# Byte masks of the quantised weights moved from VectorE to ScalarE, down steps that wait for the remainders only at their last product, and rewritten orders

## The chip, the cores and the metric

The kernel runs on one core of one Trainium2 chip. The metric is the device time of one execution in microseconds. It was run three times; the median is 339.18 us. TensorE (PE) does the matmuls, VectorE (DVE), ScalarE (ACT) and GpSimd (POOL) the element-wise work, and SyncE's queue (SP) issues nearly all DMAs. Each engine works through its own instruction list in order and meets the others at semaphores.

## The reference, cut to what matters

Two transformer layers on four sequences of 256 tokens with 256 features, each: attention, residual, layer norm, gated feed-forward, residual, layer norm.

```
x = layernorm(x + L0_attn(x));  x = layernorm(x + L0_ffn(x))     # 32 query heads of 8, 8 key heads
x = layernorm(x + L1_attn(x));  x = layernorm(x + L1_ffn(x))     # 16 query heads of 16, 8 key heads

# layer 0's feed-forward: weights rounded to float8_e4m3fn and back
wq = w.astype(float8_e4m3fn).astype(float32);  y = (x @ wq) * scale
# layer 1's feed-forward: weights are looked up, w = lut[idx], 16 entries
h = silu(gate(x)) * up(x);  out = down(h)
```

## The kernel before, in words

**Jobs.** A job j is one sequence in one layer: jobs 0 to 3 are layer 0, jobs 4 to 7 layer 1. Each job is cut into steps. TensorE's are q and kv (projections), max (scores only to find each query's maximum, 16 units a job in layer 0, 8 in layer 1), mt (turns the maxima), score (scores again, with the maximum subtracted), pv (probabilities times values), turn, back, wo (the end of attention), tr (turns x), gu (gate and up, six chunks) and down (six chunks). Every step has partner steps on other engines: VectorE reduces the maxima (max) and forms the hidden chunk (gu), ScalarE does the exponentials (score), the tanh (gu) and most copies out of PSUM, GpSimd forms remainders.

**Split operands.** To keep float32 accuracy, a rounded part and a remainder are multiplied separately. For the hidden chunk i of the down product, ScalarE writes the rounded part HH (step hsplit, semaphore `h_hi`), then GpSimd subtracts and writes the remainder HL (semaphore `h_parts`). Layer 1 has W1 (the rounded weights) and W1L (what the rounding left), so its down chunk has three products for each of two token tiles t: W1·HH, W1·HL, W1L·HH. W1L goes through DRAM: step lutlow writes LO to `dw`, and ten reload steps of 216 KB bring it back as W1L.

**Quantised weights of layer 0 (step q8, twelve chunks of 384 columns).** SP loads a chunk into RAW (ldq8, two buffers, each reloaded when `q8_used` says so). ScalarE rounds it twice to float8, as it is (Q8A) and times 0.25 (Q8B), and converts both back (QA in TH, QB in HF). VectorE makes a byte mask BIG from Q8B's top exponent bit (L1064) and copies QB over QA where it is set (L1068). GpSimd writes the result to W0 (q8w, L685, semaphore `q8_done`). All twelve have to be done before layer 0's first gu step.

**Looked-up weights of layer 1 (ten chunks of 432 columns).** lutix (ScalarE) makes bytes of the indices, lutbits (VectorE) four bit masks, lut1 (GpSimd L747 and, for the first six chunks, ScalarE L910) the eight first-level values, lut2, lut3 and lut4 (VectorE L1092) select among them, lutlow copies W1 (ScalarE L917) and subtracts (GpSimd L736).

**Stacks.** Queries and keys are split in three bfloat16 parts. ScalarE writes part 0 from PSUM (q, kv: L764, L783), GpSimd the difference (qdif, kdif: L690, L695), ScalarE part 1 (qmid, kmid: L791, L796), GpSimd part 2 (q, kv: L656, L660). SP copies the parts into QS and KS (qstack, kstack: L550, L557; six DMAs each for a job), and a job's first max step waits for all twelve. The negated maxima are added as two rows of QS by SP's mt step (L593), for which the job's first score step waits.

**Order.** What an engine does after what is written out by hand in five strings, `ORDER["PE"]` and so on. A number after @ is the PSUM bank of the three (FB) that filler steps share: a step waits until the bank's previous holder has been read. In-order issue makes a step that waits hold up all behind it.

**The last job's down (j = 7)** writes to MM instead of FB. It runs over t outside and products inside, and after chunk 5 it signals `down_half` for each t, so that VectorE can begin its layer norm on the first token tile.

Of the kernel before, what the change touches and what calls it, by code (L numbers as in the profile page):

```python
# [10 lines left out]
I32 = mybir.dt.int32  # L11
# [71 lines left out]
def unit0(j):  # L83
# [180 lines left out]
def two_layer_kernel(nc, x, xt, wq0, wk0, wv0, wo0, gate0, up0, down0, gs0, us0, ds0,  # L264
# [7 lines left out]
    with ExitStack() as ctx:  # L272
# [139 lines left out]
        x_last = sem("x_last")  # L412
        var_last = sem("var_last")
        rstd_last = sem("rstd_last")
        down_half = sem("down_half")
        th_done = sem("th_done")
        q8_cast = sem("q8_cast")
        big_done = sem("big_done")
        x_sum = sem("x_sum")
        lut_steps = sem("lut_steps")  # L420
        q8_used = sem("q8_used")
        q8_done = sem("q8_done")
        x_hi = sem("x_hi")
        h_new = sem("h_new")
# [943 lines left out]
```

## Time and profile before

| | |
|---|---|
| median of 3 runs | 339.18 us (337.5 to 340.79) |
| the profiled execution | 339.6 us, of which the span of its instructions is 337.4 us |
| TensorE busy | 287.7 us (85%) |
| VectorE, ScalarE, GpSimd busy | 248.9, 234.1, 197.6 us |
| mean granted TensorE clock | 0.939 of full speed |

Times in all views are microseconds from the span's start. The 2.2 us between the span and the time are start and end of the execution. Busy shares are averages over stages with different limits, so the stages have to be read one by one.

### The profile page before, as it was taken

How to read it: one execution, taken by the hardware profiler on the slowest of the kernel's cores; microseconds unless marked ns; L12 is line 12 of the kernel's file. 1: busy time of each engine (PE TensorE's matmuls, PEld its weight loads, DVE VectorE, ACT ScalarE, POOL GpSimd, SP SyncE). 2: the span in 40 equal slices, each digit the busy share in tenths (PEclk: the TensorE clock that was granted, in tenths of full speed). 3: DMA queues.
4: the chain of work that ended last, by engine and by line, in shares of the span. 5: the costliest groups of instructions: out<-in, count | busy, mean ns of one | idle time of the engine just before them, and what ended most of it. 6: DMA issues, size and time to landing. Idle time of an engine off the chain costs nothing.

```text
span 337.4 us, 7111 instructions
## 1 busy us (share of the span) xinstructions
PE 287.7 (85%) x2608; PEld 202.0 (60%) x2608; DVE 248.9 (74%) x408; ACT 234.1 (69%) x432; POOL 197.6 (59%) x273
## 2 busy tenths in 40 slices
PE   8512675766877889999999999999997999999993
PEld 6400242222343547767656776777877778889993
DVE  7378989899789999998985967586665566425344
ACT  2649589999799777876776977886774566654340
POOL 5548272533527759797698565664563533646654
PEclk9955587899799999999999999999999999999997
DMA  7340733232700232100321110052085000000001
GB/s 203 105 130 27 223 89 115 73 115 81 205 3 28 54 121 55 35 2 4 106 64 54 47 52 22 3 148 76 20 231 104 1 4 3 32 2 31 2 2 62
DMA packets 24888, 23.06 MB, mean 68 GB/s; under 512 B 3558, under 2 KB 24854, under 8 KB 24854
## 3 DMA queue, kind: packets, MB, share of 16 engines
q1 hardware_dynamic: 24854, 22.61, 23.6%
q8 instruction: 21, 0.34, 0.4%
q14 instruction: 13, 0.11, 0.1%
HBM read 10.47 MB, written 3.26 MB: 41 GB/s over the span
## 4 chain that ended last, share of the span: by engine, by line
PE 63%; ACT 15%; DVE 10%; issue 7%; POOL 2%; DMA 2%; POOLq 0%; SPq 0%; ACTq 0%; DVEq 0%
PE FB L1286 16%; PE PV L1229 10%; PE FB L1311 7%; PE MM L1174 7%; ACT PB L863 5%; PE SC L1208 4%; PE SC L1203 4%; PE FB L1258 4%; ACT LV L910 3%; DVE LV L1092 3%; DVE MX L980 2%; PE FB L1128 2%; PE FB L1267 2%; PE FB L1241 2%; DVE QS L935 2%
## 5 line engine op out<-in xcount | busy, mean ns | idle before, releaser
L980 DVE TENSOR_REDUCE MX<-MM 128x4 f32<-128x1024 f32 x96 | 117.2, 1221 | 37.7 <-PE MM L1174 37.1
L863 ACT ACTIVATE PB<-SC 128x1024 f32<-128x1024 f32 x96 | 98.0, 1021 | 24.2 <-PE SC L1203 15.4
L1174 PE MATMUL MM<-KS,QS 62*128 62x256 bf16 (+1 forms) x384 | 47.4, 292 | 27.2 <-DVE MX L980 18.1
L729 POOL TENSOR_TENSOR HL<-HF,HH 128x256 fp32r<-128x256 f32 (+1 forms) x48 | 36.7, 774 | 32.3 <-ACT HH L840 32.2
L1229 PE MATMUL PV<-PB,VP 128*32 128x256 f32 x768 | 51.5, 391 | 0.0
L1174 PEld LDWEIGHTS MM<-KS,QS 62*128 62x128 bf16 (+1 forms) x384 | 19.7, 97 | 51.0 <-DVE MX L980 31.6
L1092 DVE COPY_PREDICATED LV<-LB,LV 128x1728 f32<-128x1728 uint8 (+2 forms) x30 | 39.1, 1304 | 6.6 <-ACT LV L910 6.4
L747 POOL TENSOR_SCALAR LV<-LB,LD,LT 128x432 f32<-128x432 uint8 x56 | 38.6, 704 | 6.9 <-DVE LD L1055 6.7
L1286 PE MATMUL FB<-XH,W 128*128 128x256 f32 x192 | 42.5, 303 | 0.0
L1286 PE MATMUL FB<-XL,W 128*128 128x256 f32 x192 | 38.5, 282 | 0.0
L1048 DVE SCALAR_TENSOR_TENSOR AA<-TH,FB 128x256 f32<-128x256 f32 (+1 forms) x48 | 20.0, 417 | 22.7 <-ACT TH L854 18.6
L1203 PE MATMUL SC<-QS,KS 64*128 64x256 bf16 x256 | 25.7, 280 | 12.0 <-ACT PB L863 10.2
L1286 PEld LDWEIGHTS FB<-XH,W 128*128 128x128 f32 x192 | 30.3, 190 | 4.2 <-issue 2.7
L1229 PEld LDWEIGHTS PV<-PB,VP 128*32 128x32 f32 x768 | 20.8, 110 | 18.8 <-issue 8.9
L1286 PEld LDWEIGHTS FB<-XL,W 128*128 128x128 f32 x192 | 29.5, 189 | 0.1
L840 ACT ACTIVATE HH<-HF 128x256 fp32r<-128x256 f32 (+1 forms) x48 | 19.3, 414 | 8.1 <-DVE HF L1051 8.1
L736 POOL TENSOR_TENSOR LO<-LV,W 128x432 f32<-128x432 f32 x10 | 11.0, 1099 | 23.7 <-ACT W L917 23.7
L1203 PEld LDWEIGHTS SC<-QS,KS 64*128 64x128 bf16 x256 | 8.6, 96 | 26.1 <-ACT PB L863 17.9
L1128 PE MATMUL FB<-XT,WQ 128*128 128x256 f32 x64 | 19.5, 440 | 1.3 <-ACT KR L786 0.9
L1311 PE MATMUL FB<-W,HH 128*128 128x256 f32 (+1 forms) x84 | 19.5, 313 | 0.0
L1208 PE MATMUL SC<-QS,KS 98*128 98x512 bf16 x64 | 19.2, 382 | 0.0
L854 ACT ACTIVATE TH<-FB 128x256 f32<-128x256 f32 (+1 forms) x24 | 9.0, 379 | 14.5 <-PE FB L1286 14.4
(107 smaller groups left out, 569.1 us busy)
## 6 DMA issues: line engine op xcount, KB each, us to landing
QS<-QP SPq DMA_DIRECT2D x48, 128.0 KB, 2.4
IX<-in_idx SPq DMA_DIRECT2D x10, 216.0 KB, 2.9
dw<-LO SPq DMA_DIRECT2D x10, 216.0 KB, 2.2
W1L<-dw SPq DMA_DIRECT2D x10, 216.0 KB, 3.0
KS<-KP SPq DMA_DIRECT2D x24, 64.0 KB, 2.0
XT<-in_xt SPq DMA_DIRECT2D x4, 256.0 KB, 3.3
X<-in_x SPq DMA_DIRECT2D x4, 256.0 KB, 2.9
RAW<-in_gate SPq DMA_DIRECT2D x4, 192.0 KB, 2.9
```

What stands on the lines that cost most here:

```text
L729: pool.tensor_tensor(HL[0:r, i, :], HF[0:r, c % 2, :], HH[0:r, i, :].bitcast(F32), ALU.subtract).then_inc(h_parts, 1)
L747: ins = pool.tensor_scalar(LV[:, i, :], LB[:, 0, :], LD[:, i:i + 1], LT[:, 2 * i:2 * i + 1], ALU.mult, ALU.add)
L863: act.activation(PB[:, quad % PB_QUADS, kt, :, :], SC[:, :, :], ACT.Exp, scale=DH[layer(j)] ** -0.5).then_inc(exp_done, 1)
L980: dve.tensor_reduce(mx, MM[:, :, :].rearrange("p (f i) s -> p f i s", f=2), axis=AX.X, op=ALU.max).then_inc(max_red, 1)
L1092: ins = dve.copy_predicated(LV[:, 0:LUT // 2:2 * gap, :], mask, LV[:, gap:LUT // 2:2 * gap, :])
L1128: ins = pe.matmul(bank[:, m * S:(m + 1) * S], WQ[l][:, t, m:D:2], XT[:, b, t, :], start=t == 0, stop=t == DT - 1)
L1174: ins = pe.matmul(MM[:, 2 * f + i, :], QS[lo:lo + r, j % NST, qs + h, qt * P:(qt + 1) * P], keys(j)[lo:lo + r, j % NST, ks, :], start=True ...
L1203: ins = pe.matmul(SC[:, place(j, c), :], keys(j)[lo:lo + r, j % NST, ks, kt * P:(kt + 1) * P], QS[lo:lo + r, j % NST, qs + u % 4, :], star ...
L1208: ins = pe.matmul(SC[:, 2 * f:2 * f + 2, :], keys(j)[lo:lo + r, j % NST, ks, kt * P:(kt + 1) * P], QS[lo:lo + r, j % NST, qs:qs + 2, :], s ...
L1229: ins = pe.matmul(PV[32 * c:32 * c + 32, r % 2, :], v, PB[:, quad % PB_QUADS, kt, place(j, c), :], start=part == 0, stop=part == (3, 1)[la ...
L1286: ins = pe.matmul(bank[:, w * S:(w + 1) * S], ffn_up(l, w, t, i)[part], xs[:, t, :], start=k == 0, stop=k == len(products) - 1)
L1311: ins = pe.matmul(bank[:, t * D:(t + 1) * D], hs[0:rows(l, i), i, t * P:(t + 1) * P], ffn_down(l, i)[part], start=i + k + t == 0, stop=(i, ...
```

## The change

1. **Mask (step q8).** VectorE's bitwise_and on Q8B with its semaphore `big_done` goes. ScalarE makes BIG instead, as Abs(0.25·Q8B) converted to bytes, before it converts Q8A and Q8B back. VectorE's q8 step is the predicated copy alone. ScalarE now waits for `q8_used` too, right behind its wait for `q8_done`, which GpSimd gives only after it has itself seen `q8_used`.
2. **Down.** A down step begins on `h_hi`; the products are reordered so that W·HL is last, and `h_parts` is waited for just before it. In the last job's down the products are outside and t inside, so the two `down_half` signals come from the last two matmuls.
3. **Memsets.** GpSimd's clearing of VP0 moves behind NHALF, as a step "ones.0" that is the first of its order.
4. **Orders.** All five are rewritten. The multiset of steps is the same but for ones.0. Most steps move by three places or fewer; the larger moves are at the start and around the last jobs.

```diff
                     if c >= 1:
                         act.wait_ge(q8_cast, c)
-                        act.wait_ge(big_done, c)
                     act.activation(Q8A, RAW[:, c % 2, :], ACT.Copy, saturate=False)
                     act.activation(Q8B, RAW[:, c % 2, :], ACT.Copy, scale=0.25, saturate=False).then_inc(q8_bytes, 1)
                     act.wait_ge(q8_bytes, c + 1)
                     if c >= 1:
                         act.wait_ge(q8_done, c)
+                        act.wait_ge(q8_used, c)
+                    act.activation(BIG[:, :], Q8B, ACT.Abs, scale=0.25)
                     act.activation(QA, Q8A, ACT.Copy)
                     act.activation(QB, Q8B, ACT.Copy, scale=4.0).then_inc(q8_cast, 1)
...
                     c = step[1]
-                    dve.wait_ge(q8_bytes, c + 1)
-                    if c >= 1:
-                        dve.wait_ge(q8_used, c)
-                    dve.tensor_scalar(BIG[:, :].bitcast(I32), Q8B.bitcast(I32), 0x40404040, None,
-                                      ALU.bitwise_and).then_inc(big_done, 1)
-                    dve.wait_ge(big_done, c + 1)
                     dve.wait_ge(q8_cast, c + 1)
                     dve.copy_predicated(QA, BIG[:, :], QB).then_inc(q8_used, 1)
...
-                    pe.wait_ge(h_parts, 6 * j + i + 1)
+                    pe.wait_ge(h_hi, 6 * j + i + 1)
...
-                    products = ((0, HH), (0, HL), (1, HH))[:2 + l]
+                    products = ((0, HH), (1, HH))[:1 + l] + ((0, HL),)
...
-                        for t in range(TT):
-                            for k, (part, hs) in enumerate(products):
+                        for k, (part, hs) in enumerate(products):
+                            if k == l + 1:
+                                pe.wait_ge(h_parts, 6 * j + i + 1)
+                            for t in range(TT):
...
                     for k, (part, hs) in enumerate(products):
+                        if k == l + 1:
+                            pe.wait_ge(h_parts, 6 * j + i + 1)
                         for t in range(TT):
```

Of the orders, the lines on which the prediction draws (start of ScalarE, GpSimd, SP and VectorE; then, without a heading, SP's and last TensorE's lines around the last job's first max step):

```diff
     "ACT": (
-        "lutix.0 q8.0 q.0 kv.0 qmid.0 lut1.0.2 kmid.0 lut1.0.3 lutlow.0 lutix.1 q.1 lutix.2 lut1.1.2 lut1.1.3 qmid.1 "
-        "q8.1 kv.1 kmid.1 q8.2 q8.3 q8.4 lutlow.1 mt.0.0 q8.5 lut1.2.2 lut1.2.3 score.0.0 lutix.3 score.0.1 score.0.2 "
+        "lutix.0 q.0 kv.0 kmid.0 qmid.0 lut1.0.2 lut1.0.3 kv.1 lutix.1 q.1 lutlow.0 q8.0 q8.1 lut1.1.2 lut1.1.3 kmid.1 "
+        "lutix.2 qmid.1 q8.2 q8.3 q8.4 lutlow.1 mt.0.0 q8.5 lut1.2.2 lut1.2.3 score.0.0 lutix.3 score.0.1 q.2 score.0.2 "
...
     "POOL": (
-        "ones.4 lut1.0.0 qdif.0 lut1.0.1 kdif.0 q.0 kv.0 lutlow.0 qdif.1 q8w.0 lut1.1.0 lut1.1.1 q.1 kdif.1 q8w.1 kv.1 "
+        "ones.0 ones.4 qdif.0 kdif.0 lut1.0.0 lut1.0.1 kv.0 q.0 qdif.1 lutlow.0 q8w.0 lut1.1.0 lut1.1.1 kdif.1 q8w.1 "
...
     "SP": (
-        "ldq8.0 ldq8.1 ldix.0 ldx.0 load.0 ldxt.1 qstack.0.0 ldix.1 kstack.0.0 qstack.0.1 qstack.0.2 kstack.0.1 "
-        "kstack.0.2 ldx.1 ldix.2 ldq8.2 ldq8.3 kstack.1.1 ldix.3 ldix.4 ldxt.2 ldq8.4 qstack.1.1 ldxt.3 lutlow.0 ldq8.5 "
+        "ldix.0 ldix.1 load.0 ldix.2 ldxt.1 qstack.0.0 kstack.0.0 ldxt.2 kstack.0.1 qstack.0.1 kstack.0.2 qstack.0.2 "
+        "ldq8.0 ldq8.1 ldx.0 ldix.3 ldx.1 ldx.2 ldq8.2 ldq8.3 ldxt.3 ldq8.4 kstack.1.1 ldq8.5 lutlow.0 qstack.1.0 "
...
     "DVE": (
-        "lutbits.0 scales lut2.0 lut3.0 lut4.0 q8.0 max.0.0 lutbits.1 max.0.1 max.0.2 max.0.3 q8.1 max.0.4 lut2.1 "
+        "lutbits.0 scales lut2.0 lut3.0 lut4.0 max.0.0 max.0.1 lutbits.1 q8.0 max.0.2 max.0.3 q8.1 max.0.4 lut2.1 "
...
-        "kstack.6.2 reload.0 reload.1 mt.5.1 mt.6.0 reload.2 reload.3 reload.4 kstack.7.0 reload.5 reload.6 reload.7 "
-        "reload.8 reload.9 qstack.7.0 qstack.7.1 kstack.7.1 kstack.7.2 qstack.7.2 mt.6.1 mt.7.0 mt.7.1 out.4 out.5 "
+        "qstack.6.2 mt.5.1 reload.0 reload.1 reload.2 reload.3 reload.4 reload.5 reload.6 reload.7 mt.6.0 kstack.7.0 "
+        "kstack.7.1 qstack.7.0 kstack.7.2 qstack.7.1 qstack.7.2 reload.8 reload.9 mt.6.1 mt.7.0 mt.7.1 out.4 out.5 "
...
-        "wo.5.0@0 max.6.7 back.5.1@2 score.6.1 gu.4.0.0@1 wo.5.1 gu.4.0.1 gu.4.1.0@2 gu.4.1.1 score.6.2 gu.4.2.0@1 "
-        "gu.4.2.1 gu.4.3.0@0 max.7.0 mt.6.1@2 score.6.3 gu.4.3.1 gu.4.4.0@2 gu.4.4.1 gu.4.5.0@1 max.7.1 down.4.0@0 "
+        "wo.5.0@0 max.6.7 back.5.1@2 score.6.1 gu.4.0.0@1 wo.5.1 score.6.2 gu.4.0.1 gu.4.1.0@2 gu.4.1.1 max.7.0 "
+        "mt.6.1@0 score.6.3 gu.4.2.0@1 gu.4.2.1 gu.4.3.0@2 max.7.1 gu.4.3.1 gu.4.4.0@0 gu.4.4.1 max.7.2 score.6.4 "
```

Counted in ScalarE's order up to its first gu step (gu.0.0), two score steps stand directly behind each other at five places before (0.1 and 0.2, 0.8 and 0.9, 0.14 and 0.15, 1.8 and 1.9, 1.10 and 1.11) and at one after (1.10 and 1.11); everywhere else another step lies between.

## Rows read from the trace of the kernel before

**Rows 1.** Busy time of each engine by stretch: length, PE, PEld, DVE, ACT, POOL, granted clock, DMA share, GB/s

```profile
22.00:44.00 22.00, 10.25 (x51) 3.82 (x49) 19.93 (x28) 14.83 (x34) 12.20 (x15) 0.50 0.41 125
44.00:111.00 67.00, 48.13 (x488) 21.56 (x487) 59.49 (x75) 61.91 (x107) 32.64 (x43) 0.92 0.31 89
111.00:127.00 16.00, 13.96 (x154) 8.52 (x152) 15.30 (x21) 11.53 (x20) 10.49 (x15) 1.00 0.33 96
127.00:254.00 127.00, 126.92 (x1203) 91.51 (x1203) 99.47 (x165) 96.45 (x173) 89.32 (x120) 1.00 0.23 62
254.00:260.00 6.00, 4.25 (x35) 3.73 (x35) 3.46 (x11) 2.29 (x5) 2.24 (x3) 1.00 0.54 111
260.00:331.00 71.00, 71.00 (x623) 62.25 (x622) 35.18 (x82) 38.20 (x78) 37.22 (x58) 1.00 0.03 9
```

**Rows 2.** The first 24 us in order of time: start, duration, instruction, idle before it

```profile
8.53 1.10 PE L1153 MATMUL FB<-WV,XT 128*128 128x64 f32 x8
...
9.72 0.58 ACT L764 ACTIVATE QP<-FB 128x512 bf16<-128x512 f32 x1
...
14.59 0.63 ACT L791 ACTIVATE QP<-QR 128x512 bf16<-128x512 f32 x1 [3.07 <-POOL QR L690]
...
15.89 0.66 POOL L695 TENSOR_TENSOR KR<-KR,KP 64x256 f32<-64x256 f32 x1
16.51 1.15 POOL L656 TENSOR_TENSOR QP<-QR,QP 128x512 bf16<-128x512 f32 x1
...
16.90 1.37 ACT L910 ACTIVATE LV<-LB,LT,LD 128x432 f32<-128x432 uint8 x2
...
18.36 1.82 SPq L557 DMA_DIRECT2D KS<-KP  x3
...
18.36 3.90 DVE L1092 COPY_PREDICATED LV<-LB,LV 128x1728 f32<-128x1728 uint8 x3 [6.12 <-ACT LV L910]
...
21.62 0.61 PE L1174 MATMUL MM<-KS,QS 62*128 62x256 bf16 x4 [7.21 <-DMA KS<-KP]
...
22.15 0.20 DVE L1064 TENSOR_SCALAR BIG<-AA 128x96 int32<-128x96 int32 x1
22.39 0.59 DVE L1068 COPY_PREDICATED TH<-BIG,HF 128x384 f32<-128x384 uint8 x1
22.87 1.21 DVE L980 TENSOR_REDUCE MX<-MM 128x4 f32<-128x1024 f32 x1
```

**Rows 3.** ScalarE from 44 us, in order of time: one q8 step and its neighbours

```profile
52.22 0.51 ACT L887 ACTIVATE AA<-RAW 128x384 fp8e4<-128x384 f32 x1
52.63 0.51 ACT L888 ACTIVATE AA<-RAW 128x384 fp8e4<-128x384 f32 x1
...
53.61 0.51 ACT L893 ACTIVATE HF<-AA 128x384 f32<-128x384 fp8e4 x1
54.02 1.00 ACT L863 ACTIVATE PB<-SC 128x1024 f32<-128x1024 f32 x1
```

**Rows 4.** What ScalarE waited for from 44 to 111 us: total, times, longest

```profile
ACT PB L863 <- PE SC L1203: 4.2, 6, 1.7
```

**Rows 5.** Groups by line and shape: the one load of ScalarE's tables

```profile
L900 ACT ACT_TABLE_LOAD x1 | 1.3, 1283 | 0.7 <-PEq L1358 0.7
```

**Rows 6.** SP's queue and TensorE before the last job's first max step, in order of time

```profile
247.01 2.50 SPq L614 DMA_DIRECT2D W1L<-dw  x5
...
254.84 0.56 SPq L550 DMA_DIRECT2D QS<-QP  x1
...
259.26 0.61 PE L1174 MATMUL MM<-KS,QS 96*128 96x256 bf16 x4 [1.75 <-DMA QS<-QP]
```

**Rows 7.** DMA issues: KB each, median us to landing

```profile
QS<-QP SPq DMA_DIRECT2D x48, 128.0 KB, 2.4
```

**Rows 8.** The end, in order of time

```profile
331.19 0.28 PE L1303 MATMUL MM<-W1L,HH 48*128 48x256 f32 x1
...
331.58 0.42 DVE L1026 TENSOR_TENSOR X<-X,MM 128x256 f32<-128x256 f32 x1 [1.50 <-PE MM L1303]
```

More of the change, by code:

```diff
@@ L417, in two_layer_kernel @@
         q8_cast = sem("q8_cast")
-        big_done = sem("big_done")
         x_sum = sem("x_sum")
@@ L641, in _ @@
                                base=0, pattern=[[-1, P]], channel_multiplier=1).then_inc(const_pool, 1)
-            link(pool.memset(VP0[:, :, :, :, :], 0.0))
-            pool.memset(VP0[:, :, :, :, 24:25], 1.0).then_inc(ones_pool, 1)
             link(pool.memset(NHALF[:, :], -0.5))
@@ L646, in _ @@
                 kind = step[0]
-                if kind == "ones":
+                if kind == "ones" and layer(step[1]) == 0:
+                    link(pool.memset(VP0[:, :, :, :, :], 0.0))
+                    pool.memset(VP0[:, :, :, :, 24:25], 1.0).then_inc(ones_pool, 1)
+                elif kind == "ones":
                     link(pool.memset(VP1[:, :, :, :, :], 0.0))
@@ L1305, in _ @@
                                                 stop=(i, k) == (5, len(products) - 1))
-                            if i == 5:
-                                ins.then_inc(down_half, 1)
+                                if (i, k) == (5, len(products) - 1):
+                                    ins.then_inc(down_half, 1)
                         continue
                     for k, (part, hs) in enumerate(products):
+                        if k == l + 1:
+                            pe.wait_ge(h_parts, 6 * j + i + 1)
                         for t in range(TT):
```

206 rows, old and new, of the table ORDER are left out of this document.

## The prediction

> **What bounds the kernel now.** I read the busy times by stretch first, because one share for the whole span would mislead [rows 1]. Three regimes follow each other. From 22 to 127 us TensorE is not full: 48.1 of 67 us from 44 to 111. There ScalarE is, with 61.9 of 67 us, and VectorE nearly so with 59.5; from 22 to 44 us VectorE leads with 19.9 of 22, and TensorE runs at 0.50 of its clock, the lower of its two levels, 1.2 GHz; from 111 to 127 us VectorE has 15.3 of 16. From 127 us to 331 us TensorE does nothing but matmuls: 126.9 of 127 us, then, after one hole, 71.0 of 71. In this regime no other engine matters unless it makes TensorE wait. The hole lies in the 6 us from 254 (4.25 busy). The third regime is the tail after the last matmul, some 6 us of layer norm and output.
>
> So the time is the moment at which the packed part begins, plus a fixed amount of matmul work, plus holes, plus the tail. The change neither adds nor removes matmuls. A gain can come from the first 127 us, from the hole, or from the tail, and I go through these three. The sum is made against the profiled execution, 339.6 us with a span of 337.4; it stands 0.4 us above the median of the three runs, which is inside their spread of 3.3 us. About 1% is what a measurement of this kernel can tell from no change.
>
> **The start, up to the first max step.** VectorE's first selection (lut2.0) begins at 18.36 after 6.1 us of waiting for ScalarE's last table pair, which ends at 18.27, and TensorE's first max step at 21.62 after 7.2 us of waiting for the key stack [rows 2]. ScalarE reaches its first q step at 9.72, behind q8.0, and waits 3.07 us for GpSimd's difference at 14.59 because GpSimd does a table first. The new orders take q8.0 out and put both differences ahead of the tables. Then ScalarE's q step is done when kv's matmuls end at 9.63; kv takes about 0.85 us (what followed q before), GpSimd's kdif 0.66, kmid and qmid about 1.0, the two table pairs 1.37 each: 9.7 + 0.85 + 0.66 + 1.0 + 2.74 is about 15.0 in place of 18.3. VectorE's three selections take 3.90, to 18.9. On GpSimd the differences (1.15 as the row of the same shape, and 0.66) run while it would be idle, so its last stack part, which ended at 16.51 + 1.15 + 0.66 = 18.3, ends at 16.5. Before, SP's last stack issue ended at 20.2 and the step began 1.4 us later; now the issue ends near 17.2 and the step begins at 18.7 to 19. The first reduction is then at about 19.5 instead of 22.87: 3.3 us earlier.
>
> **The mask.** On VectorE each of the twelve BIG steps goes, from 22.15 to the copy's start at 22.39: 0.24 us, 2.9 us in all. On ScalarE twelve Abs come. The profile has no Abs; the nearest rows are the conversions of the same 384 float8 columns, which follow each other every 0.41 to 0.43 us inside a step and have a duration of 0.51 [rows 3]. I take 0.42, since ScalarE's instructions overlap and the step's pitch is what its queue pays: 5.0 us in all. From below the price is nothing, where ScalarE waits anyway, from above 0.51 each, 6.1 us. The added wait costs nothing by itself: GpSimd gives `q8_done` only behind `q8_used`, and ScalarE waited for that already. What queues behind it is all of ScalarE. This trade is bad on its face, 5.0 us onto the engine with 61.9 of 67 us. Five of the Abs (q8.0 to q8.4) lie before 44 us, where ScalarE has 14.8 of 22 us, and are mostly hidden; q8.5 stands before the first exponential, six more (2.5 us) are in the full stretch.
>
> **Carried to 111 us.** Until the first exponential I keep 2.5 of the 3.3 us. What is lost: q8.1's back conversions wait for GpSimd's first write, and that for VectorE's q8.0, now behind two max steps; and at half clock the projection steps between the max steps weigh double. From there six Abs cost 2.5. Against it stands what ScalarE waits for: 4.2 us in six waits for scores, up to 1.7 long [rows 4]. Each time two exponentials follow each other directly, the second waits about half a microsecond, since there is one score buffer; the new order has one such pair instead of five, which gives back 4 times 0.5, 2.0 us. The long wait of 1.7 us has another maxima row transfer and filler matmuls at half clock behind it; I count half, 0.9. So at 111 us ScalarE is 2.5 - 2.5 + 2.0 + 0.9 = 2.9 us earlier. VectorE has to follow for the stretch to 127 us, where it is the bound: it keeps some 1.7 to 2.5 us of the start and gains 0.24 for each of the last seven BIG (1.7), so it does. **Front: -2.9 us**, with bounds of -5 (all waits gone) and +2.5 (nothing of the start carried, six Abs paid).
>
> **The hole.** TensorE stands 1.75 us before the last job's first max step, because the last stack part, issued at 254.84, lands 4.4 us later, behind five W1L transfers of 216 KB whose issue alone took SP 2.50 us at 247 [rows 6]; the median of such a stack transfer is 2.4 us [rows 7]. In the new order two of the ten reloads come behind the stacks and eight before the sixth job's maxima rows, well ahead. Of what is moved past them, SP's mt.6.0 is now queued behind eight reloads; score.6.0, which needs it, stands a whole group of steps later in TensorE's order, so I cost that at nothing, and at 1 us if the backlog is still there. SP saves up to 2.5 us, so the last issue is at 252.3 to 254.8 and lands at 254.7 to 257.2. But the new order wants it three gu units earlier: 623 matmuls in 71.00 us are 0.114 each [rows 1], 18 of them 2.1 us, so at 257.5 - 2.1 = 255.4. The hole is then 0 to 1.8 us. I take 0.35, for a **gain of 1.4 us**: the issue hangs on GpSimd's part rather than on SP. The gain goes wholly into the end, as all behind is packed.
>
> **Down and the tail.** In the packed part TensorE never waits for `h_parts` (126.9 of 127 and 71.0 of 71 us), so the later wait frees nothing: 0. In the last step the first token tile's last product was third of six and is now fifth. VectorE began at 331.58, 0.39 us after the start of the third, so it begins two matmuls later [rows 8]: **+0.2 us**. If the cover were gone and the last remainder late, the old form would pay GpSimd's 0.7 us there and the new one less; that case gains nothing here. The memset's move changes nothing: GpSimd idles until 12 us.
>
> **The sum.** 337.4 - 2.9 - 1.4 + 0.2 = 333.3 us of span, with the 2.2 us around it 335.5 us. That assumes that the rewritten orders bring no new wait of TensorE in the 200 packed microseconds. Few moves there are large and VectorE, ScalarE and GpSimd have a quarter or more free, but each is in order; I allow up to 2 us.
>
> **A load of tables.** ScalarE loads its function tables once, in 1.28 us [rows 5]. If Abs needed another set than Exp and Tanh, each q8 step between exponentials would pay two loads: 24 times 1.28 is 31 us, 366 us in all. The Trainium skill's page ScalarE: Activation LUTs, section "Table sets: the hidden batching unit", says that cheap functions, abs among them, are in every set, and lists abs and tanh in the one anchored on exp. By that rule there is no load. No run here shows it yet. The same page gives some 2.7 us for a switch with its drain; by that the 24 would cost about 64 us.
>
> **The rivals.**
> *ScalarE's price is what counts (slower).* If the start's 3.3 us end in waits before 44 us (half clock, RAW transfers that need `q8_used` and so VectorE's order), every Abs lies on the chain and the hole stays: 339.6 + 5.0 + 0.2 = 344.8 us. For it: ScalarE has 61.9 of 67 us. Against it: it waits 4.2 us of the rest, and the start's waits are long ones with named causes that the new orders take away. It decides where ScalarE has no idle time left before the first exponential.
> *Start lost, hole filled.* Gains and Abs cancel up to 127 us and only the hole goes: 339.6 - 1.4 + 0.2 = 338.4. For it: TensorE is itself at 14.0 of 16 us from 111 to 127.
> *More than the sum.* All 4.2 us of waits go and VectorE's 2.9 too: front -5 to -6, 332.5 or below.
> *The orders don't do what they seem to.* Another wait takes the place of each removed one: 339.4.
>
> **How the numbers follow.** Forecast 0.45, own range 333.7 to 337.3; start lost 0.25; slower by ScalarE 0.12; more than the sum 0.12; nothing moves 0.04; table loads 0.02. Faster by over 1% is below 335.8: a little over half of the forecast and all of "more", 0.38. Slower by over 1% is above 342.6: ScalarE's case, the loads and an unforeseen wait, 0.15. The rest, 0.47, lies between. The range of 332.5 to 341.5 leaves out the slower cases and the end of the best one.
>
> **What the profile after would show.** The first reduction near 19.5 us; Abs rows of about 0.5 us, twelve of them, and still one table load; ScalarE at over 63 of 67 us between its first exponential and first tanh, with fewer waits for scores; the last job's first max step without idle time, or under 0.5; TensorE packed from about 124 us on; the last step's VectorE add 0.6 us after the third matmul of six. The prediction is wrong if TensorE shows new waits after 127 us, if the first reduction is early but the first gu step is not, or if the stack still lands 4 us after its issue.

## The result and the profile after

The changed kernel takes 336.61 us (median of 13 runs, 335.58 to 337.9); the kernel before took 339.18 in 13 runs beside them. The ratio is 0.992, with a 95% interval of 0.990 to 0.994: faster, by 2.6 us. The profiled execution after takes 336.61 us with a span of 334.4 us, 3.0 us less than the span before. All differences of single places below are between profiled executions.

Busy time by stretch after, with the columns of [rows 1]: length, PE, PEld, DVE, ACT, POOL, granted clock, DMA share, GB/s.

```profile
22.00:44.00 22.00, 9.32 (x48) 3.46 (x49) 19.14 (x23) 18.92 (x41) 12.67 (x17) 0.50 0.42 125
44.00:111.00 67.00, 52.33 (x509) 24.09 (x511) 58.26 (x70) 62.36 (x109) 31.91 (x44) 0.85 0.30 85
111.00:127.00 16.00, 14.08 (x154) 8.17 (x146) 15.06 (x21) 11.71 (x20) 10.83 (x14) 1.00 0.21 52
127.00:254.00 127.00, 126.48 (x1193) 91.47 (x1190) 97.63 (x164) 96.03 (x173) 86.26 (x117) 1.00 0.25 70
254.00:260.00 6.00, 6.00 (x52) 5.62 (x51) 4.74 (x9) 3.63 (x9) 3.13 (x4) 1.00 0.05 18
260.00:328.00 68.00, 68.00 (x598) 59.36 (x596) 32.88 (x82) 35.74 (x73) 37.26 (x57) 1.00 0.03 9
```

Read it against [rows 1]. ScalarE rose from 61.9 to 62.4 of 67 us, VectorE fell from 59.5 to 58.3. The six microseconds that held 4.25 us of matmuls are full. From 127 us on TensorE is packed but for one new gap of half a microsecond. The granted clock from 44 to 111 us is 0.85 instead of 0.92: TensorE ran 19.7 us of that stretch, up to 63.7 us, at the lower of its two levels (1.2 GHz), in place of 10.2 us before. That is more time at the lower clock, and yet the stretch is done sooner.

The start, in order of time, to be held against [rows 2]:

```profile
12.63 2.65 ACT L911 ACTIVATE LV<-LB,LT,LD 128x432 f32<-128x432 uint8 x4
...
12.68 2.75 POOL L747 TENSOR_SCALAR LV<-LB,LD,LT 128x432 f32<-128x432 uint8 x4 [0.92 <-DVE LD L1056]
...
15.39 0.66 POOL L660 TENSOR_TENSOR KP<-KR,KP 64x256 bf16<-64x256 f32 x1
15.46 5.47 DVE L1087 COPY_PREDICATED LV<-LB,LV 128x1728 f32<-128x1728 uint8 x3 [2.59 <-POOL LV L747]
16.02 1.14 POOL L656 TENSOR_TENSOR QP<-QR,QP 128x512 bf16<-128x512 f32 x1
...
17.23 0.53 SPq L549 DMA_DIRECT2D QS<-QP  x1
...
19.59 0.61 PE L1169 MATMUL MM<-KS,QS 62*128 62x256 bf16 x4 [3.48 <-DMA QS<-QP]
20.82 1.21 DVE L981 TENSOR_REDUCE MX<-MM 128x4 f32<-128x1024 f32 x1
```

ScalarE's four tables end at 15.28, the selection begins at 15.46 (18.36 before), but it takes 5.47 us instead of 3.90. So the first reduction is 2.05 us earlier and not 3.3. In the view of one tile (VectorE's instructions on LV up to 23 us; shortest, median and longest of the three in ns) the whole of the longer time lies in the first of the three, lut2.0; first the kernel before,

```profile
L1092 DVE COPY_PREDICATED LV<-LB,LV x3: 646/1117/2070, 18.4 to 21.6; 128x1728 f32<-128x1728 uint8 x1, 128x864 f32<-128x864 uint8 x1, 128x432 f32<-128x432 uint8 x1
```

then the kernel after:

```profile
L1087 DVE COPY_PREDICATED LV<-LB,LV x3: 642/1122/3633, 15.5 to 20.3; 128x1728 f32<-128x1728 uint8 x1, 128x864 f32<-128x864 uint8 x1, 128x432 f32<-128x432 uint8 x1
```

The same 128x1728 selection took 3.63 us with two GpSimd subtractions beside it, and 2.07 without. 

One q8 step after, ScalarE in order of time, against [rows 3]; then the line's group; then the waits against [rows 4] and the table load against [rows 5]:

```profile
51.59 0.52 ACT L886 ACTIVATE AA<-RAW 128x384 fp8e4<-128x384 f32 x1
52.00 0.51 ACT L887 ACTIVATE AA<-RAW 128x384 fp8e4<-128x384 f32 x1
52.55 0.52 ACT L892 ACTIVATE BIG<-AA 128x384 uint8<-128x384 fp8e4 x1
52.98 0.51 ACT L893 ACTIVATE TH<-AA 128x384 f32<-128x384 fp8e4 x1
```

```profile
L892 ACT ACTIVATE BIG<-AA 128x384 uint8<-128x384 fp8e4 x12 | 6.3, 522 | 2.7 <-POOL W L685 2.4
L901 ACT ACT_TABLE_LOAD x1 | 1.3, 1283 | 0.7 <-PEq L1357 0.7
```

```profile
ACT PB L863 <- PE SC L1198: 2.5, 4, 0.9
```

The Abs has the 0.52 us of its neighbours and takes 0.43 of the queue (52.55 to 52.98), so twelve are 5.2 us. There is still one table load. ScalarE waits for scores four times instead of six, 1.7 us less in sum.

The one new gap, and the last job's first max step with SP's issues ahead of it, against [rows 6]:

```profile
165.96 0.39 PE L1169 MATMUL MM<-KS,QS 62*128 62x256 bf16 x4 [0.52 <-DVE MX L981]
...
249.53 1.84 SPq L549 DMA_DIRECT2D QS<-QP  x3
251.42 1.08 SPq L613 DMA_DIRECT2D W1L<-dw  x2
...
253.71 0.61 PE L1169 MATMUL MM<-KS,QS 96*128 96x256 bf16 x4
```

The max step shows no idle time. The end, against [rows 8]:

```profile
327.61 0.50 PE L1300 MATMUL MM<-W,HH 48*128 48x256 f32 x2
...
328.19 0.40 PE L1300 MATMUL MM<-W,HL 48*128 48x256 f32 x2
328.57 0.42 DVE L1027 TENSOR_TENSOR X<-X,MM 128x256 f32<-128x256 f32 x1 [2.20 <-PE MM L1300]
```

Where the 3.0 us came from, following the same steps through both profiles: first reduction -2.05, first exponential -2.2, first gu step (its tanh on ScalarE) 111.50 to 109.23 (-2.3), 127 us -2.15, from 172 us on -1.4 (the gap of 0.52 and what lies around it), behind the last job's first max step -3.2 (the hole's 1.75), last addition 331.58 to 328.57 (-3.0).

Such differences of one pair of profiles carry a spread. Experiments 2, 3, 6, 9 and 10 below have the same program as the kernel before up to the first gu step, which they reach at 113.3, 111.6, 112.4, 111.5 and 112.3 us, against 111.5 before. Experiment 5 has the program of the kernel after up to there and reaches it at 108.2, against 109.2. The averages are 112.1 and 108.7, so the front may be worth more than the 2.3 us of this pair; and a difference under 1 us at that place, between two profiles, shows nothing by itself.

### The profile page after: what moved, and what is told of

Its sections match the earlier page's. It is cut to its first block, busy times and chain, and to the rows that moved or that the text cites. A ratio compares the mean times of both kernels' runs of the same rounds, so it can differ in the third digit from the quotient of the medians.

```text
span 334.4 us, 7088 instructions
## 1 busy us (share of the span) xinstructions
PE 290.2 (87%) x2608; PEld 202.9 (61%) x2608; DVE 247.3 (74%) x396; ACT 239.1 (72%) x444; POOL 197.0 (59%) x273
## 4 chain that ended last, share of the span: by engine, by line
PE 70%; DVE 11%; ACT 10%; issue 4%; POOL 2%; DMA 1%; POOLq 0%; SPq 0%; ACTq 0%; DVEq 0%
PE FB L1281 18%; PE PV L1224 11%; PE MM L1169 9%; PE FB L1310 8%; DVE MX L981 5%; PE SC L1203 4%; ACT PB L863 4%; PE SC L1198 4%; PE FB L1253 3%; PE FB L1123 3%; DVE LV L1087 3%; PE FB L1262 2%; PE FB L1143 2%; PE FB L1148 2%; PE FB L1236 1%
## 5 line engine op out<-in xcount | busy, mean ns | idle before, releaser
L1169 PE MATMUL MM<-KS,QS 62*128 62x256 bf16 (+1 forms) x384 | 48.5, 299 | 25.2 <-DVE MX L981 21.7
L1224 PE MATMUL PV<-PB,VP 128*32 128x256 f32 x768 | 52.2, 391 | 1.0 <-ACT ST L878 0.5
L1087 DVE COPY_PREDICATED LV<-LB,LV 128x1728 f32<-128x1728 uint8 (+2 forms) x30 | 40.2, 1340 | 2.9 <-POOL LV L747 2.6
L1198 PE MATMUL SC<-QS,KS 64*128 64x256 bf16 x256 | 26.7, 289 | 7.3 <-ACT PB L863 6.1
L1224 PEld LDWEIGHTS PV<-PB,VP 128*32 128x32 f32 x768 | 20.3, 110 | 19.6 <-issue 8.4
L1198 PEld LDWEIGHTS SC<-QS,KS 64*128 64x128 bf16 x256 | 9.2, 98 | 20.2 <-ACT PB L863 11.9
L1123 PE MATMUL FB<-XT,WQ 128*128 128x256 f32 x64 | 18.7, 430 | 1.0 <-DMA XT<-in_xt 1.0
L685 POOL TENSOR_SCALAR W<-TH 128x384 fp32r<-128x384 f32 x12 | 6.4, 532 | 21.8 <-DVE TH L1063 21.8
L1203 PE MATMUL SC<-QS,KS 98*128 98x512 bf16 x64 | 19.2, 382 | 0.0
L1281 PE MATMUL FB<-XH,W1L 128*128 128x256 f32 x96 | 19.1, 280 | 0.0
L1310 PE MATMUL FB<-W,HH 128*128 128x256 f32 (+1 forms) x84 | 18.9, 306 | 0.0
```

The lines of the kernel that those rows point to most:

```text
L1087: ins = dve.copy_predicated(LV[:, 0:LUT // 2:2 * gap, :], mask, LV[:, gap:LUT // 2:2 * gap, :])
L1123: ins = pe.matmul(bank[:, m * S:(m + 1) * S], WQ[l][:, t, m:D:2], XT[:, b, t, :], start=t == 0, stop=t == DT - 1)
L1169: ins = pe.matmul(MM[:, 2 * f + i, :], QS[lo:lo + r, j % NST, qs + h, qt * P:(qt + 1) * P], keys(j)[lo:lo + r, j % NST, ks, :], start=True ...
L1198: ins = pe.matmul(SC[:, place(j, c), :], keys(j)[lo:lo + r, j % NST, ks, kt * P:(kt + 1) * P], QS[lo:lo + r, j % NST, qs + u % 4, :], star ...
L1203: ins = pe.matmul(SC[:, 2 * f:2 * f + 2, :], keys(j)[lo:lo + r, j % NST, ks, kt * P:(kt + 1) * P], QS[lo:lo + r, j % NST, qs:qs + 2, :], s ...
L1224: ins = pe.matmul(PV[32 * c:32 * c + 32, r % 2, :], v, PB[:, quad % PB_QUADS, kt, place(j, c), :], start=part == 0, stop=part == (3, 1)[la ...
```

## The experiments

Each ratio is to the kernel before on the same chip: 339.42 us there for the first four (35 runs), 339.77 for the next four (22 runs), 339.18 for the last three (23 runs).

**1. Mask alone.** The kernel before, orders untouched, with the diff's first part.

```diff
-                        act.wait_ge(big_done, c)
...
+                        act.wait_ge(q8_used, c)
+                    act.activation(BIG[:, :], Q8B, ACT.Abs, scale=0.25)
...
-                    dve.tensor_scalar(BIG[:, :].bitcast(I32), Q8B.bitcast(I32), 0x40404040, None,
```

> The orders and the down steps of before, with the masks made by ScalarE. Theory (the mask edit is a burden that the new orders outweigh): slower than before by 1 to 4 us, 340 to 343, as q8.0 alone delays the first stack by 0.4 us and the six Abs between the first exponential and the first tanh stand on the full ScalarE. Rival (VectorE's relief of 2.9 us is what makes the changed kernel faster): faster by 1 to 2 us, 337 to 338.

342.58 us (340.38 to 345.27), ratio 1.009 [1.005, 1.013]: 3.2 us slower. Its windows:

```profile
44.00:111.00 67.00, 49.70 (x460) 21.37 (x460) 55.76 (x64) 61.86 (x110) 27.35 (x39) 0.82 0.30 89
```

The first reduction is at 22.6 (22.9 before), the first exponential 0.6 us later, the first gu step 4.0 us later (115.5), the hole 1.28. So the price arises between the first exponential and the first gu step, where six of the Abs stand, and VectorE's freed time doesn't make up for it. The clock in this profile is lower too (0.82 against 0.92), so the 4.0 is not Abs alone; the 3.2 of the medians is the better number.

**2. Down alone.** The kernel before with the diff's down part.

```diff
-                    pe.wait_ge(h_parts, 6 * j + i + 1)
+                    pe.wait_ge(h_hi, 6 * j + i + 1)
...
-                    products = ((0, HH), (0, HL), (1, HH))[:2 + l]
+                    products = ((0, HH), (1, HH))[:1 + l] + ((0, HL),)
...
```

> Before with the down edit alone. Theory (nothing in the packed part waits for the remainders; the first token tile of the last step comes two matmuls later): the span is 0 to 0.3 us longer, VectorE's last add starts 0.6 us after the third last-step matmul instead of 0.39. Rival (waiting for the remainders costs somewhere that the views do not show): faster by over 0.5 us.

339.93 us, ratio 0.999 [0.995, 1.003]: nothing. SP, TensorE and the end:

```profile
256.13 0.56 SPq L550 DMA_DIRECT2D QS<-QP  x1
...
259.10 0.61 PE L1174 MATMUL MM<-KS,QS 96*128 96x256 bf16 x4
...
330.81 0.50 PE L1305 MATMUL MM<-W,HH 48*128 48x256 f32 x2
...
331.77 0.42 DVE L1026 TENSOR_TENSOR X<-X,MM 128x256 f32<-128x256 f32 x1 [1.76 <-PE MM L1305]
```

The tail's 0.2 us is there: the addition begins 0.96 us after the last chunk does, as in the kernel after (327.61 to 328.57), where the old form has 0.73. A second thing shows. In this execution the front was 1.8 us late (first gu step at 113.3), and the hole is gone: the max step still starts at 259.1. It is not the late front alone that fills it, since the stack's last issue moved with the front (256.13 for 254.84). But the transfer landed 2.9 us after its issue, where it took 4.4 in the kernel before:

```profile
L550 SPq DMA_DIRECT2D QS<-QP x1: 558/558/558, 256.1 to 256.1; - x1
DMA to landing us min/median/max: 2.9/2.9/2.9
```

And experiment 1, with a front 4.0 us late, still had a hole of 1.28.

**3. Reloads late alone.** The kernel before with the late part of SP's order of the kernel after, from mt.5.1 on.

```diff
-        "kstack.6.2 reload.0 reload.1 mt.5.1 mt.6.0 reload.2 reload.3 reload.4 kstack.7.0 reload.5 reload.6 reload.7 "
-        "reload.8 reload.9 qstack.7.0 qstack.7.1 kstack.7.1 kstack.7.2 qstack.7.2 mt.6.1 mt.7.0 mt.7.1 out.4 out.5 "
+        "kstack.6.2 mt.5.1 reload.0 reload.1 reload.2 reload.3 reload.4 reload.5 reload.6 reload.7 mt.6.0 kstack.7.0 "
+        "kstack.7.1 qstack.7.0 kstack.7.2 qstack.7.1 qstack.7.2 reload.8 reload.9 mt.6.1 mt.7.0 mt.7.1 out.4 out.5 "
```

> Before with SP's late lines of the changed kernel alone (eight reloads before mt.6.0, the last job's stacks before the last two reloads). Theory: the 1.75 us hole of TensorE before the last job's first max step goes, and all of it reaches the end: 337.4 to 337.7 in place of 339.2. Rival (the last stack part is bound by GpSimd's remainder and not by the reloads, the gain comes from TensorE's order): hole still 1 to 1.75 us, time within 0.3 us of before.

342.29 us (339.57 to 346.78), ratio 1.006 [1.002, 1.011]: slower, and the hole stays.

```profile
244.06 8.81 SPq L557 DMA_DIRECT2D KS<-KP  x5
...
255.57 1.85 SPq L550 DMA_DIRECT2D QS<-QP  x3
...
259.25 0.61 PE L1174 MATMUL MM<-KS,QS 96*128 96x256 bf16 x4 [1.71 <-DMA QS<-QP]
```

SP sits 8.8 us in the key stack: kstack.7.1 now comes first and needs kmid.7, which ScalarE's old order makes at 251.18. The third of the last stack issues starts near 256.8 and lands 2.4 us later, the usual time [rows 7]; so the transfers are quick now, and the issue is late instead. My explanation of the hole was half of it. Why the median is slower no profile shows: the profiled run (339.61) is the second fastest of the twelve.

**4. After with VectorE's masks.** The diff's first part undone in the kernel after.

> The changed kernel with the masks made by VectorE again, orders as changed. Theory (mask edit a burden): faster than the changed kernel's 336.6 by 0.5 to 2.5 us, 334 to 336. Rival (VectorE's relief is the gain): slower than the changed kernel by 1 us or more, 337.6 and up.

336.39 us, ratio 0.992 [0.988, 0.995], the same as the kernel after; span 334.0. In the new orders the mask's move is worth nothing, in the old ones it costs 3 us.

**5 and 6. Orders, cut at about 205 us.** Each engine's list is taken from one kernel up to the cut and from the other behind it.

```
# in words, not the lines of the edit
5: the kernel after; ORDER["PE"][318:], ["ACT"][205:], ["DVE"][168:], ["SP"][89:], ["POOL"][117:]
   are the same steps in the order of the kernel before
6: the kernel before, with the late orders of the kernel after; masks and down as before
```

> The changed kernel, but from about 205 us on (from max.5.0 on TensorE) all five orders are those of before. Theory (the late orders as a whole fill the hole before the last job's first max step, worth 1.75 us): 338.0 to 338.6, with a hole of 1 to 2 us in the profile. Rival (the hole only takes up what the front leaves, the whole gain is the front's): 336.6 to 337.

> Before, but with the late orders of the changed kernel (from max.5.0 on TensorE), old masks, old down. Theory: the hole goes, 337.3 to 338 in place of 339.4. Rival: within 0.5 us of before.

Number 5: 338.34 us, ratio 0.996 [0.993, 1.000]. Two gaps come, in a front that was 1.0 us ahead of the kernel after's:

```profile
203.57 0.29 PE L1182 MATMUL FB<-IDB,MS 128*128 128x128 bf16 x2 [0.73 <-ACT ON L874]
...
256.86 0.61 PE L1173 MATMUL MM<-KS,QS 96*128 96x256 bf16 x4 [0.89 <-DMA QS<-QP]
```

Number 6: 339.61 us, ratio 1.002 [0.998, 1.005]. Its profile has no hole at the max step (256.77, no idle time), a front 0.9 us late, and a span of 337.1.

```profile
256.77 0.61 PE L1178 MATMUL MM<-KS,QS 96*128 96x256 bf16 x4
```

So the late orders do remove the hole in a profile, with the old front as well; in the median they give 1.7 us behind the new front (336.6 against 338.3, on two chips) and nothing that can be measured behind the old one. Experiment 4 (with VectorE's masks), on the chip of number 5, has 336.4, some 2 us less than that. The early orders, with the mask and the down edit, give 0.4%, at the edge of the interval. So the late orders count behind the new front only, and the early ones are just visible.

**7. GpSimd's parts first.** The kernel after, one move in the first job.

```diff
-        "ones.0 ones.4 qdif.0 kdif.0 lut1.0.0 lut1.0.1 kv.0 q.0 qdif.1
+        "ones.0 ones.4 qdif.0 kdif.0 lut1.0.0 kv.0 q.0 lut1.0.1 qdif.1
```

> The changed kernel with GpSimd's third stack parts of job 0 (kv.0, q.0) before its second pair of tables, so that they no longer run beside VectorE's first selection. Theory (the selection took 3.6 us instead of 2.1 because GpSimd subtracted beside it): it starts 1.8 us later, at about 17.2, and takes 2.1 to 2.2 us, so that the first reduction comes at about the same time, 20.8 to 21.1. Rival (its length has another cause): it again takes about 3.6 us and the first reduction comes at 22.5 or later.

336.36 us in one run, span 334.0. The selection in the view of one tile:

```profile
L1087 DVE COPY_PREDICATED LV<-LB,LV x3: 1116/1440/2077, 17.2 to 20.5; 128x1728 f32<-128x1728 uint8 x1, 128x864 f32<-128x864 uint8 x1, 128x432 f32<-128x432 uint8 x1
```

and in order of time, where GpSimd's next difference comes to lie beside the last selection:

```profile
14.65 1.15 POOL L656 TENSOR_TENSOR QP<-QR,QP 128x512 bf16<-128x512 f32 x1
15.79 1.38 POOL L747 TENSOR_SCALAR LV<-LB,LD,LT 128x432 f32<-128x432 uint8 x2
...
19.46 1.96 POOL L690 TENSOR_TENSOR QR<-QR,QP 128x512 f32<-128x512 f32 x1 [2.28 <-ACT QR L767]
```

With the subtractions out of the way lut2.0 is back at 2.08 us. But it starts 1.75 us later, behind the second table, and the last selection, of 432 columns, now has GpSimd's difference beside it and takes 1.44 us for 0.64. The move shifted the meeting of the two engines more than it took it away. So the first reduction is at 21.81, 1.0 us later than in the kernel after, and yet the first gu step is 0.4 us earlier (108.9). That doesn't show that a microsecond at the start is worth nothing: in the stretch from 44 us the clock was 0.91 here and 0.85 in the kernel after, and experiment 5, with the start of the kernel after and 0.91, has its first gu step at 108.2, 0.6 us ahead of this one.

**8. Busy start.** The kernel after with 36 and then nine times 5 matmuls of an identity into SC ahead of the first max steps, to see whether a TensorE that is busy early is granted the higher clock early. What they write to SC is written over.

```diff
+                    if j == 0 and u <= 9:
+                        for _ in range(36 if u == 0 else 5):
+                            pe.matmul(SC[:, 0, 0:P], IDN[:, :], IDN[:, :], start=True, stop=True)
```

> The changed kernel with extra matmuls of the identity into the still unused score buffer: 36 before the first max step and 5 before each of the next nine, nothing reads them. Theory (the start's gain is eroded between 40 and 85 us because TensorE runs at the lower clock from 19 to 64 us): the clock stays at 2.4 GHz over more of that stretch and the first gu step comes 0.5 to 2 us earlier, 334.5 to 336. Rival (the erosion is ScalarE's six Abs and VectorE's load, whatever the clock): 336.3 to 337.5.

345.11 us in 6 runs, ratio 1.017 [1.011, 1.024]. The windows:

```profile
22.00:44.00 22.00, 19.64 (x159) 16.91 (x159) 11.99 (x12) 11.74 (x25) 8.69 (x11) 0.95 0.22 68
44.00:111.00 67.00, 51.13 (x486) 24.15 (x486) 59.68 (x71) 63.49 (x118) 28.66 (x40) 0.87 0.35 98
```

The clock from 22 to 44 us went from 0.50 to 0.95, with TensorE 19.6 of 22 us busy instead of 9.3. But the 36 extra matmuls stand behind the wait for the stack, so they didn't fill TensorE's idle time: they began at 20.44 and took 10.18 us. The first reduction is at 31.0, 10.2 us later, and the span is 9.4 us longer than after, so the clock's price can't be read from it: inconclusive for that. What it shows is that a delay of this size does reach the end: 8.9 us at the first exponential, 8.7 at the first gu step, 9.4 in the span. There is also a wait of 0.58 us for the stack at the last job's first max step again; in the kernel after the stack lands only 0.6 us before TensorE comes to it (253.1 for 253.7).

**9 and 10. Key part early, with and without the late reloads.** The kernel before with two moves; number 9 has SP's two lines of experiment 3 as well.

```diff
-   ACT  ... kv.7 q.7 back.5.0 stage.5.1 tr.4.0 score.6.0 qmid.7 back.5.1 kmid.7 score.6.1
+   ACT  ... kv.7 q.7 kmid.7 back.5.0 stage.5.1 tr.4.0 score.6.0 qmid.7 back.5.1 score.6.1
-   POOL ... kdif.7 qdif.7 xd.4 q.7 kv.7 xadd.5
+   POOL ... kdif.7 qdif.7 kv.7 xd.4 q.7 xadd.5
```

> The kernel before with three moves only: ScalarE's kmid.7 right behind q.7, GpSimd's kv.7 before xd.4, and SP's last two order lines of the kernel after (eight reloads ahead of the last job's stacks, two behind). Theory that the hole of 1.7 us before the last job's first max step needs ScalarE's and GpSimd's key parts early: SP's key stack is then released near 247.5 instead of 251.6, the last stack issue starts near 252.3 (GpSimd's last query part ends at 252.2) instead of 254.8, and the hole shrinks to 0 to 0.3 us; span 335.8 to 336.2, time about 338. Rival, that only TensorE's rewritten order fills it: the hole stays at 1.5 us or more, time as before.

> As the run with the late reloads, but SP's order is that of the kernel before (all ten W1L transfers ahead of the query stacks). If the backlog of the reloads plays no part, the hole is as short as in the other run (within 0.3 us), since SP's issue then hangs on GpSimd's last query part at 252.2. If the backlog is what the last stack lands behind, the landing stays over 4 us after its issue and the hole at 1 us or more.

Number 9, SP and TensorE:

```profile
243.99 4.26 SPq L561 DMA_DIRECT2D KS<-KP  x5
...
251.02 1.85 SPq L554 DMA_DIRECT2D QS<-QP  x3
...
257.32 0.61 PE L1178 MATMUL MM<-KS,QS 96*128 96x256 bf16 x4
```

Number 10, in its one run 340.01 us:

```profile
247.77 2.50 SPq L618 DMA_DIRECT2D W1L<-dw  x5
...
255.60 0.56 SPq L554 DMA_DIRECT2D QS<-QP  x1
...
259.67 0.61 PE L1178 MATMUL MM<-KS,QS 96*128 96x256 bf16 x4 [1.33 <-DMA QS<-QP]
```

The four cases of the hole stand side by side: neither move 1.75 us, reloads late alone 1.71, key part early alone 1.33, both 0. TensorE's rewritten order is not needed. With the reloads ahead the last stack takes 4.07 us from issue to max step (255.60 to 259.67), as before (4.4); with the key part late, SP's issue waits. Either alone is enough to keep the hole, since each makes the same stack late.

The reloads ahead make it late in two ways. In number 10 SP issues five of them before the query stacks, in 2.50 us, and the last stack issue, less the 0.8 us by which the front was late, comes at 254.8 against 252.3 in number 9. By an estimate from the usual 2.4 us [rows 7] it would still land at 257.2, just ahead of TensorE (257.5); the slow landing makes the hole. And this landing is not the same in every execution. For the last stack transfer in each profile:

| reloads | run | last issue | landed after, us | hole, us |
|---|---|---|---|---|
| ahead | before | 254.8 | 4.4 | 1.75 |
| ahead | 10 | 255.6 | 4.0 | 1.33 |
| ahead | 1 | 259.0 | 3.7 | 1.28 |
| ahead | 5 | 253.3 | 3.6 | 0.89 |
| ahead | 2 | 256.1 | 2.9 | 0 |
| late, key part late | 3 | 256.9 | 2.3 | 1.71 |
| late, key part early | 9, 6, after | 252.3, 253.9, 250.8 | 2.3 to 2.4 | 0 |

Number 9 has the same front as the profile before and a span 2.0 us shorter (335.4). Its median is 338.7 us, ratio 0.999 [0.995, 1.002]: less than the profile's 2.0. The table offers a reason: the profile before has the largest hole of the five with the reloads ahead, whose average is 1.05 us, so closing it should be worth less in the median than in that pair. That is argued, not shown, run by run.

**11. A combination.** The kernel after with VectorE's masks, experiment 7's move, and the token tile outside again in the last job.

```diff
-                        for k, (part, hs) in enumerate(products):
-                            if k == l + 1:
-                                pe.wait_ge(h_parts, 6 * j + i + 1)
-                            for t in range(TT):
+                        for t in range(TT):
+                            for k, (part, hs) in enumerate(products):
+                                if k == l + 1 and t == 0:
+                                    pe.wait_ge(h_parts, 6 * j + i + 1)
```

> The kernel after with VectorE's masks of before, GpSimd's key and query parts of the first job ahead of its second table step, and in the last job's sixth down chunk the token tile outside again. Each part was worth 0.2 to 0.4 us in a profile: the mask 0.4 of span, GpSimd's order 0.3 with it or less, the tail 0.2. Expected 335.9 us, against the kernel after's 336.6; VectorE's last add 0.5 us behind the third last product but one, that is the tail 0.2 us shorter. Rival: the gains of the front are swallowed, 336.4, with the tail's 0.2 alone kept.

337.74 us (336.65 to 339.01), ratio 0.995 [0.992, 0.998]: no better than the kernel after, rather worse. The tail is as hoped: the addition begins 0.73 us after the last chunk does, 0.23 less than after.

```profile
328.91 0.39 PE L1306 MATMUL MM<-W,HH 48*128 48x256 f32 x1
...
329.64 0.42 DVE L1027 TENSOR_TENSOR X<-X,MM 128x256 f32<-128x256 f32 x1 [1.94 <-PE MM L1306]
```

The front is 1.7 us behind that of experiment 4 (first gu step 110.6 against 108.9). In the profile the first projection took 2.87 us, for 1.90 in experiment 7, and GpSimd's first difference beside VectorE's set-up 3.08 us, for 1.15 in the kernel after:

```profile
5.09 2.87 PE L1129 MATMUL FB<-XT,WQ 128*128 128x256 f32 x8
...
9.17 3.08 POOL L691 TENSOR_TENSOR QR<-QR,QP 128x512 f32<-128x512 f32 x1 [3.83 <-ACT QR L768]
```

Why the projection was slow was not tested. No version here beats the kernel after beyond what was measured; experiment 4 equals it.

## Why the prediction held, step by step

The forecast of 335.5 us is 1.1 us below the median; the time lies inside the range and inside the forecast's own range. Against the profiled pair the 1.1 us are a front worth 0.6 less, 0.9 lost again between 127 and 172 us, and a hole worth 0.35 more. Of the prediction's own signs of being wrong one came, a new wait of TensorE after 127 us. The signs of all terms were right. Their sizes:

- **The start, -3.3: measured -2.05.** The step "VectorE's three selections take 3.90, to 18.9" failed. The selection's start was right to half a microsecond (15.46 for 15.0), its length was not: lut2.0 took 3.63 us because the same reordering put GpSimd's kv.0 and q.0, from 15.39 to 17.16, beside it. I had counted GpSimd's share of the start as work in its idle time and had not asked what runs beside it. Experiment 7 takes them away and has 2.08. This step explains 0.6 of the 1.3 us that were missed. The rest lies in the stack: GpSimd's last part ended at 17.16 and not at 16.5, since its tables begin only at 12.68 and end at 15.43, and the first max step began at 19.59 and not at 18.7 to 19; the reduction can't come before that step's matmuls, at 20.2. The Trainium skill's page SBUF — State Buffer, section "SBUF: two separate sides", says that VectorE and GpSimd share a pair of ports, for which they contend when, for one, the VectorE instruction has two inputs in SBUF and the GpSimd one reads SBUF; the one that starts first then holds the pair for its whole instruction while the other is blocked. The trace agrees, if the mask counts as the selection's second input: from GpSimd's end at 17.16 the usual 2.07 us lead to 19.23, and the selection ended at 19.09.
- **Front at 111 us, -2.9: measured -2.3, and -1.4 by 172 us.** What I kept of the start to the first exponential was 2.5; it is 2.2. ScalarE's waits for scores fell by 1.7 of the 2.9 that I gave back. What I left out is that the front goes on being spent after 127 us: a max step at 165.96 waits 0.52 us for VectorE. The sum's allowance for new waits, up to 2 us, was where it went. Over the profiles that share each front the gain at the first gu step averages 3.4, so the 2.3 of this pair doesn't show that the 2.9 was too much.
- **The mask, 5.0 us on ScalarE.** The price of one was right (0.43 of queue, 5.2 in all). Alone in the old orders it costs 3.2 us at the end, in the new orders 0 (experiments 1 and 4). The trade was bad on its face, as said; the orders hide it. Experiment 4 reaches the first exponential 0.8 us later than the kernel after and the first gu step 0.3 earlier, but the clock differs between these profiles (0.90 against 0.85 from 44 to 111 us). Experiment 5, with ScalarE's masks, the same start and 0.91, is at its first gu step 0.7 us before experiment 4. So there the moved mask costs nothing that can be measured; why the new orders hide it so fully is not settled.
- **The hole, -1.4: measured -1.75.** The size was right by luck, since two causes hold it up and I named one and leaned on another, and since the hole is 0 to 1.75 us in the five profiles with the reloads ahead. I put the late landing down to the reloads, and experiment 10 agrees (4.07 us from issue to use). But I took it that "the issue hangs on GpSimd's part rather than on SP", and wrote that SP saves up to 2.5 us. Experiment 3 shows SP saving nothing, because kmid.7 on ScalarE was late. That ScalarE and GpSimd make the key part earlier in the new orders I had not read at all; experiment 9 shows that it is the other half.
- **Down, 0, and the tail, +0.2:** right. Experiment 2 measures no change and +0.2 (0.96 for 0.73 us).
- **No table load:** right, one load of 1.28 us as before.
- **The rivals.** "ScalarE's price is what counts" is what experiment 1 makes of the old orders (342.6 us). "Start lost, hole filled", 338.4, fell: 2.2 us of the start reached 127 us.

## What to carry to other kernels

When a reordering starts an instruction earlier, price it by what now runs beside it: a VectorE selection beside GpSimd subtractions took 3.63 us and not 2.07. A stall before a stack of transfers can have two causes of nearly equal lateness, of which removing one shows nothing; list every issue on the queue and the work that each waits for, and test the moves in all four combinations. A stall that ends with a transfer can differ from execution to execution (0 to 1.75 us here, with the landing at 2.9 to 4.4 us), so read it from several profiles before pricing it. An order that hides one extra operation makes an edit's price depend on it (3.2 us or nothing for the same twelve Abs).

## What the runs showed of the hardware

- GpSimd and VectorE slow each other in both directions: VectorE's 128x1728 selection 3.63 for 2.07 us, its 128x432 selection 1.44 for 0.64, GpSimd's 128x512 subtraction 1.96 for 1.15 us beside a selection (both experiment 7) and 3.08 beside VectorE's set-up (experiment 11).
- The stretches in which TensorE is granted its lower level differ between executions, also where the program is the same. Experiment 5 has the program of the kernel after in this part, and its stretches are 11.7 to 18.5, 21.9 to 45.8 and 52.6 to 62.9 us, with the first gu step 1.0 us earlier. The others: 16.6 to 43.9, 54.1 to 60.9 and 84.8 to 88.2 us before; 19.4 to 63.7 after; 19.2 to 46.5 and 53.4 to 63.6 in experiment 4. In experiment 8, with TensorE 19.6 of 22 us busy, the granted clock of that stretch was 0.95, and 0.50 to 0.56 before, after and in experiments 1, 2, 4, 5, 6 and 7, where it was busy 8.3 to 10.3 us.
- The last stack transfer of 128 KB landed 2.3 to 2.4 us after its issue with the W1L transfers moved away (after, experiments 3, 6 and 9) and 2.9 to 4.4 us with ten of 216 KB ahead of it (before, experiments 1, 2, 5 and 10).
- An activation with Abs from float8 to bytes takes 0.52 us for 384 columns, as a copy does.
